# A cross-attention kernel: the values of unit c-2 ahead of the scores of unit c+1

## The reference

```python
q = _split_heads(hidden_states @ w_q, HEADS)
k = _split_heads(text @ w_k, HEADS)
v = _split_heads(text @ w_v, HEADS)
out_text = _merge_heads(_sdpa(q, k, v))
k_ip = _split_heads(ip_h @ w_k_ip, HEADS)
v_ip = _split_heads(ip_h @ w_v_ip, HEADS)
out_ip = _merge_heads(_sdpa(q, k_ip, v_ip, mask=mask_ip))
out = out_text + IP_SCALE * out_ip
out = out @ w_out + b_out
out = out + residual
```

## Time and profile before

| | |
|---|---|
| median of 3 runs | 404.87 us |
| lowest and highest | 404.58, 407.13 us |
| profiled execution, its own time | 405.48 us |
| its span | 403.7 us |
| granted TensorE clock | 1.00 |
| TensorE busy | 394.1 us (98%) |
| VectorE busy | 335.8 us (83%) |
| ScalarE, GpSimd busy | 129.2, 155.8 us |
| mean DMA rate | 181 GB/s |

### The profile page before, as it was taken

The page is one execution under the profiler, slowest core; times in us unless marked ns, Lnnn a source line. Parts: engine busy times, 40 slices in busy tenths (PEclk is TensorE's granted clock), DMA queues, the critical chain, the costliest instruction groups (busy, mean ns, idle before and its releaser), DMA issues.

```text
span 403.7 us, 10795 instructions
## 1 busy us (share of the span) xinstructions
PE 394.1 (98%) x4452; PEld 290.9 (72%) x4452; DVE 335.8 (83%) x458; ACT 129.2 (32%) x196; POOL 155.8 (39%) x128
## 2 busy tenths in 40 slices
PE   8899999999999999999999999999999999999996
PEld 7688878567776777777776776777776767776765
DVE  4559679899998998999999889999999898999523
ACT  4236344453333322432323322433323322232100
POOL 0336622687426423373226533372226532222200
PEclk9999999999999999999999999999999999999999
DMA  8999936675657455664558455754467454454555
GB/s 282 369 374 331 215 100 206 187 209 163 175 159 223 121 146 143 211 175 119 150 147 250 119 151 137 207 174 130 137 175 230 132 139 128 131 145 119 164 168 189
DMA packets 42849, 72.96 MB, mean 181 GB/s; under 512 B 10544, under 2 KB 10672, under 8 KB 42800
## 3 DMA queue, kind: packets, MB, share of 16 engines
q1 hardware_dynamic: 37680, 67.02, 54.7%
q10 hardware_dynamic: 5120, 5.25, 5.4%
HBM read 35.53 MB, written 10.49 MB: 114 GB/s over the span
## 4 chain that ended last, share of the span: by engine, by line
PE 78%; DVE 8%; DMA 5%; SPq 4%; issue 2%; ACT 1%; ACTq 1%; DVEq 0%
PE ps L637 57%; PE ps L668 8%; PE ps L682 8%; PE ps L712 3%; SPq L259 2%; DMA out_tiles<-res 2%; DVE text_max L501 2%; DVE prob L507 2%; DMA wk_raw<-in_w_k 2%; DVE o_lo L543 1%; ACTq L403 1%; PE ps L718 1%; DMA res<-in_x 1%; ACT prob L395 1%; SPq L279 1%
## 5 line engine op out<-in xcount | busy, mean ns | idle before, releaser
L357 POOL TENSOR_TENSOR prob<-prob,rden 128x1104 f32<-128x1104 f32 x40 | 82.2, 2055 | 202.7 <-DVE rden L530 202.7
L637 PE MATMUL ps<-x_hi,wq_hi 128*128 128x512 f32 x200 | 83.1, 416 | 0.9 <-DVE x_lo L599 0.9
L637 PE MATMUL ps<-o_hi,wo_hi 128*128 128x512 f32 x200 | 79.0, 395 | 0.8 <-DVE o_lo L543 0.5
L637 PE MATMUL ps<-x_lo,wq_hi 128*128 128x512 f32 x200 | 78.7, 394 | 0.0
L637 PE MATMUL ps<-x_hi,wq_lo 128*128 128x512 f32 x200 | 78.1, 390 | 0.0
L637 PE MATMUL ps<-o_lo,wo_hi 128*128 128x512 f32 x200 | 77.9, 390 | 0.0
L637 PE MATMUL ps<-o_hi,wo_lo 128*128 128x512 f32 x200 | 77.9, 389 | 0.0
L395 ACT ACTIVATE prob<-prob 128x1232 f32<-128x1232 f32 x40 | 50.0, 1250 | 68.8 <-DVE prob L518 68.8
L537 DVE STREAM_TRANSPOSE prob_t<-prob 128x1536 f32<-128x1536 f32 x40 | 70.6, 1766 | 0.1
L501 DVE TENSOR_REDUCE text_max<-ps 128x16 f32<-128x1104 f32 x40 | 52.1, 1303 | 18.9 <-PE ps L668 18.8
L637 PEld LDWEIGHTS ps<-x_hi,wq_hi 128*128 128x128 f32 x200 | 37.5, 187 | 36.1 <-issue 28.4
(11 more groups left out here) (58 smaller groups left out, 349.1 us busy)
## 6 DMA issues: line engine op xcount, KB each, us to landing
prob_k<-prob_t SPq DMA_DIRECT2D x320, 64.0 KB
stage<-in_x SPq DMA_DIRECT2D x38, 256.0 KB, 3.3
res<-in_x SPq DMA_DIRECT2D x37, 256.0 KB, 2.7
out_tiles<-res SPq DMA_DIRECT2D x37, 256.0 KB, 2.3
prob_k<-prob_t ACTq DMA_DIRECT2D x160, 32.0 KB
wki_raw<-in_w_k_ip SPq DMA_DIRECT2D x5, 512.0 KB, 7.2
wk_raw<-in_w_k SPq DMA_DIRECT2D x5, 512.0 KB, 6.9
wv_raw<-in_w_v SPq DMA_DIRECT2D x5, 512.0 KB, 7.9
```

The source lines that it names most:

```text
L357: nc.gpsimd.tensor_tensor(e[:, :, 0:TEXT], e[:, :, 0:TEXT], rden[:, par, 0, :].unsqueeze(2).to_broadcast([P, QT * HG, TEXT]), ALU.mult)
L637: return nc.tensor.matmul(ps[:, bank, :], w[:, g, P * kt:P * kt + P], m[:, b, kt, :], start=(n == 0), stop=(n == 3 * KD - 1))
```

## The change

In every steady step, and in the late steps, `make_o(c - 2)` is called ahead of `make_scores(c + 1)` instead of behind it. The instructions themselves, their semaphores and the other engines' orders stay as they are. Steps 0 to 5 use `early_step` and are not touched; step 39 has no scores.

```diff
             def late_step(c):
 
+                make_o(c - 2)
                 if exists(c + AHEAD_S):
                     make_scores(c + AHEAD_S)
-                make_o(c - 2)
                 make_out(c - BEHIND_OUT)
 
             def step(c):
...
                 else:
+                    make_o(c - 2)
                     make_scores(c + AHEAD_S)
-                    make_o(c - 2)
                     make_q(c + AHEAD_Q, whole)
                     make_out(c - BEHIND_OUT)
```

## The result

The changed kernel takes 414.5 us (median of 4 runs, 413.97 to 414.96) against 405.42 us (4 runs, 404.58 to 407.13): ratio 1.0194, 95% interval 1.0167 to 1.0222. A later comparison gave 1.0185 (1.0156 to 1.0214). The profiled execution took 413.97 us with a span of 412.1; before it was 405.48 and 403.7.

What follows compares the result with a forecast made beforehand. TensorE was taken to set the pace, with longer g = 0 steps waiting for VectorE's `o_low`. Long steps 5.9, step 6 0, end 1.0, handovers 0 sum to +6.9 us on 404.87: 411.8 us (+1.7%), range 408.0 to 414.6.

Steps and rivals of the forecast that it cites:

- The ordinary step costs nothing: Steps without g = 0: swapping values and scores on TensorE leaves 8.90 us, VectorE running 0.99 us later at the same pace.
- Six long steps pay 0.99 us each, 5.9 us: Steps 11 to 36 with g = 0: the projection waits for `o_low`, delayed 0.99 us by the later scores; 5.9 us.
- The handover of values to scores costs 0.99, and the sum of handovers 0: TensorE's changes of array shape: values to scores takes 0.99 us, all handovers together add 0.
- rival of a cheap one at 0.88: Values-to-scores handover takes 0.88 instead of 0.99 us: 3.6 us less, +3.3 us, 408.2; chance 0.13.
- scores under the values: Rival at the same handover: scores start while values run, so not slower; 403.5 us at 0.25 us per step; chance 0.04.
- GpSimd keeps its phase, 0: Image shift against GpSimd's x_lo operations in long steps: both move together, 0; if phase shifted, -2.5 to +3.0 us.
- Step 6 pays nothing: Step 6: values fill TensorE's 0.71 us idle hole before the scores, `o_low(4)` stays within some 0.2 us; 0.
- The end pays 0.99 us: Last 30 us, on SP's queue: copies behind unit 38's transpose move with unit 39's scores; 0.99 us on top.
- more is lost: Rival: VectorE meets GpSimd at a worse point, or late residual loads hold `finish`; about 3 us more, 414.8; chance 0.10.
- less is lost through the signal of the scores: Rival: scores followed by a full product signal 0.2 us sooner; +5.5 us, 410.4; inside the forecast, no chance of its own.

Runs made afterwards that it cites:

- e2: Against the kernel before, values first only in the g = 0 steps (6, 11, ..., 36), scores first elsewhere: 414.03 us, ratio 1.0177.
- e5: Kernel before, with GpSimd making the lo part of x for only the first eighth of the columns: 404.5 us, ratio 0.995.
- e3: Against the kernel before, values first in steps 6 to 36, scores first in 37 and 38: 412.93 us, ratio 1.0166.
- e4: Against the kernel before, only in g = 0 steps: values first, `o_low` ahead of the maximum, ScalarE's hi parts of x behind `o_high`: 407.49 us, ratio 1.0009.
- e10: The kernel before once more, no edit, as the second pair's before: 406.94 us in its one run.
- e11: The changed kernel once more, no edit, against the kernel before: 414.36 us, ratio 1.0185.
- e6: Changed kernel, with GpSimd making the lo part of x for only the first eighth of the columns, against the kernel before: 413.16 us, ratio 1.0167.
- e8: Against the kernel before, in every step from 11 on: values first, `o_low` ahead of the maximum, hi parts behind `o_high`: 430.48 us, ratio 1.0591.
- e9: Against the kernel before, values first in steps 6, 37 and 38 alone: 408.18 us, ratio 1.0035.
- e7: Against the kernel before, only in g = 0 steps from 11 on: values first, `o_low` ahead of the maximum, hi parts behind `o_high`: 404.51 us, ratio 0.9951.
- e1: Against the kernel before, values first in all steps from 6 on except those with g = 0: 406.73 us, ratio 1.0004.

## Why the prediction was right

411.8 us was forecast, 1.7% more; 414.5 came, 1.9% more. The mechanism is the one that was forecast, but the number lies only 0.1 us inside the range (408.0 to 414.6). Against the kernel before it is +9.1 us in the first comparison and +7.5 in the second, where +6.9 was forecast; 0.55 us of the distance to 411.8 is the kernel before itself, whose median had become 405.42. Point by point:

- *The ordinary step costs nothing:* right. It stays at 8.90 us, and its maximum starts 2.23 us after the step's first product (step 24; 2.28 was forecast). The sum of all steps that are not long moved by +0.24 and -0.24 us.
- *Six long steps pay 0.99 us each, 5.9 us:* right, 5.8 and 6.5 us in the two pairs. e2, which changes these steps and step 6 alone, loses 1.77% of 406.6, 7.2 us. That 5.9 lies so near is in part luck: with GpSimd shortened the order costs 5.35 us, because in e5 TensorE is not yet held by `o_low` (in its step 21 the output starts 0.17 us behind it, where it starts 0.05 or 0.06 us behind it in the steps that wait), and 0.4 and 1.1 us come on top in the two pairs.
- *The handover of values to scores costs 0.99, and the sum of handovers 0:* right, 0.99 to 1.00 in the chains of after. The rival of a cheap one at 0.88, and that of scores under the values, are out.
- *GpSimd keeps its phase, 0:* right only roughly. In steps 16 to 36 the image shift changes by at most 0.37 us, but in step 11 it goes from 0.65 to 1.14 us in the first pair and from 0.29 to 1.34 in the second, and that step grows most (1.12 and 1.42 us). In sum over the six steps the shift changes by -0.3 and +1.5 us, where the forecast allowed -2.5 to +3.0. The prediction's reading that a lag moves this price in whole GpSimd operations is not borne out: the end of the shift falls on a boundary of theirs, but its length takes values in between, such as 0.50, 0.57, 0.83 and 1.14 us.
- *Step 6 pays nothing:* right within some tenths of a microsecond. Counted from the values of unit 3, ahead of any changed step, step 7 starts after 15.9 to 17.4 us (mean 16.5) in the six profiles with scores first there and after 16.1 to 17.5 (mean 16.7) in five with values first; e3, with its dip of the clock, took 18.9, and e4 has another order on VectorE. The forecast missed that ScalarE's four issues get longer with the new order (3.10 us or more instead of 2.72 or less), and that `o_low(4)` can then wait for `o_high(4)`.
- *The end pays 0.99 us:* the mechanism was right, the size is known only roughly. Measured from the first product of step 38, the copies of unit 38 begin 1.00, 0.63 and 0.65 us later in the three pairs (before and after, e10 and e11, e5 and e6). The end as a whole is 2.3 and 2.0 us longer in the first two pairs and 0.1 shorter in the third. Over all profiles but e8, the mean from step 38 to the end is 38.1 us in the seven with scores first there (37.2 to 38.6) and 39.3 in the five with values first (38.3 to 39.8), 1.2 apart. e9, which changes steps 6, 37 and 38 alone, loses 0.7 to 2.1 us by its interval.

Where the pairs differ stands on SP's queue. Its timeline at the end of after, answering to the earlier trace rows:

```profile
371.77 6.04 SPq L259 DMA_DIRECT2D prob_k<-prob_t  x8
...
380.10 0.34 SPq L270 DMA_DIRECT2D res<-in_x  x1
380.54 5.09 SPq L259 DMA_DIRECT2D prob_k<-prob_t  x8
...
388.38 5.90 SPq L259 DMA_DIRECT2D prob_k<-prob_t  x8
...
395.93 0.43 SPq L274 DMA_DIRECT2D out_tiles<-res  x1
399.82 0.33 SPq L270 DMA_DIRECT2D res<-in_x  x1
```

And of before, the same store and the residual load behind it:

```profile
388.22 0.43 SPq L274 DMA_DIRECT2D out_tiles<-res  x1
391.87 0.33 SPq L270 DMA_DIRECT2D res<-in_x  x1
```

Measured from the first product of step 38 (366.52 before, 372.60 after), the copies of unit 38 begin at 6.94 before and at 7.94 after: the 0.99 us of the forecast. From there on the distances were taken to stay. The last eight copies took 5.90 us to issue instead of 5.43, and the residual load behind the store started 3.89 us after it instead of 3.65 (391.87 - 388.22), so it stands at 27.22 instead of 25.35, +1.87. The copies of unit 38 also begin 0.10 us behind the residual's issue (380.10 + 0.34), where before there were 0.72 us between them: the queue itself had become as late as the transpose. The second pair has +0.63 at the copies and +1.69 at that residual, the third +0.65 and -0.03: there the last eight copies took 5.76 us with scores first and 5.27 with values first. So the greater part of the forecast shift reaches the copies in every pair, and what lies beyond it comes from the times of these issues and round trips, which go either way. Whether the order makes the end pay more than the 0.99 us is not shown.

The rival *more is lost* (414.8) is nearer to the measured number than the forecast is. Of its two grounds the first, a worse phase against GpSimd, is seen in part: step 11, and the +1.5 us of the second pair. The second, a `finish` held by late residual loads, is not seen: between 88 and 376 us neither profile has such a wait. The rest of the excess stands at the end, as far as the first two pairs of profiles tell: +2.3 and +2.0 us where 1.0 was forecast.

The rival *less is lost through the signal of the scores* is not settled. From the first product of the scores to the maximum it takes 1.23 us before and 1.25 after in the mean of the six long steps, but 1.32 and 1.16 in the second pair and 1.22 and 1.17 in the third. The 0.2 us of the rival did not come; a smaller gain is possible.

## What to carry to other kernels

In this kernel a reorder on the busiest engine was free in every step where that engine sets the pace and the other engines' slack covers the shift (8.90 us stayed 8.90), and cost nearly its full shift in each step in which that engine waits for work behind the moved product. So count those steps and multiply. What such a step loses could be bought back by moving the releasing work ahead on its own engine (e7, 0.5% under the kernel before), but only where nothing slow, here a queue of DMA issues, stood in front of it (e4, e8). Where steps of two orders alternate, look at the phase of VectorE against GpSimd before reading a ratio near 1 as no effect.

## What the runs showed of the hardware

- The image shift, a VectorE operation of 0.29 us with two inputs in SBUF, took from 0.34 us (e1) to 1.34 us (e11) in long steps where GpSimd's operations of 1.28 us ran, and its end then fell 0.15 us behind a boundary of theirs. The Trainium skill, SBUF — State Buffer, "SBUF: two separate sides", describes the shared port pair as an exclusive lock that is held for a whole instruction. The trace agrees by these ends; and with GpSimd's operations shortened (e5) the shift took 0.29 or 0.30 us in all six long steps, which were 1.8 us shorter in sum.
- Four DMA issues on ScalarE took from 2.44 to 4.80 us for copies of the same size, and eight on SP's queue from 4.95 to 6.67. In step 6 the four took 2.46 to 2.72 us in six profiles with scores first and 3.10 to 4.80 in seven with values first; why is open.
- ScalarE's computing instructions stand behind its issues: `o_high` waited 87.3 us for them between 120 and 380 us in e8.
- Eight value products of 77 x 32 tiles, followed by the scores' tiles of 32 x 64, took 0.99 to 1.00 us from their start to the next start.
